# Products of a constant matrix in TensorE's pauses, in a two-layer pair-mixing network with a recurrence and a choice of experts

## The reference, cut to what matters

```python
x = x + _L0_conv_ref(_ln_c(x), ...)   # layernorm, gated projection to 4 x 8 channels, two batched
                                       # 128x128 products per channel, layernorm over 16, gated projection
t = t + _L0_ffn_ref(_ln_t(t), ...)     # Wx, batch statistics, then y = sigmoid(Wx_t + y @ V.T) along the sequence
x = x + _L1_conv_ref(_ln_c(x), ...)   # layernorm, a and b of 32 channels each, 128x128 product per channel,
                                       # layernorm, projection, output gate
t = t + _L1_ffn_ref(_ln_t(t), ...)     # router over 8 experts, softmax, two best, their weighted projections
```

## Time and profile before

| | |
|---|---|
| median of 3 runs | 358.93 us (357.75 to 360.17) |
| the profiled execution | 357.57 us |
| its span, first to last instruction | 355.8 us |
| TensorE busy, of the span | 244.0 us |
| VectorE busy | 248.4 us |
| ScalarE busy | 121.9 us |
| GpSimd busy | 97.5 us |
| mean granted TensorE clock | 0.820 |

### The profile page before, as it was taken

How to read it: one execution, slowest core, us unless ns; L and a number is a source line. 1 busy time by engine, 2 the same in 40 slices (tenths; PEclk the granted TensorE clock), 3 DMA queues, 4 the chain that set the end, 5 groups by cost and what they waited for, 6 DMA issues and landing times.

```text
span 355.8 us, 4549 instructions
## 1 busy us (share of the span) xinstructions
PE 244.0 (69%) x1465; PEld 180.0 (51%) x1465; DVE 248.4 (70%) x467; ACT 121.9 (34%) x224; POOL 97.5 (27%) x137
## 2 busy tenths in 40 slices
PE   1283985747068598970966978934566792989994
PEld 1162774424043498960745758934555791333321
DVE  4997456778867300039997963399799599999994
ACT  3061323324324245622542544642142132121210
POOL 4013363247500393000143671003236313020000
PEclk9996988569659679996798998968596555599999
DMA  7100000000000000000000000000001981096811
GB/s 235 26 2 0 0 2 0 1 1 0 1 0 2 0 0 0 2 3 0 2 0 1 0 0 2 0 0 2 0 1 38 206 200 30 5 204 177 207 59 61
DMA packets 6633, 13.05 MB, mean 37 GB/s; under 512 B 2774, under 2 KB 3030, under 8 KB 6614
## 3 DMA queue, kind: packets, MB, share of 16 engines
q1 hardware_dynamic: 6470, 12.81, 14.2%
q10 hardware_dynamic: 144, 0.01, 0.0%
HBM read 2.32 MB, written 2.10 MB: 12 GB/s over the span
## 4 chain that ended last, share of the span: by engine, by line
PE 44%; DVE 42%; issue 5%; POOL 3%; ACT 3%; DMA 1%; SPq 0%; DVEq 0%; POOLq 0%; ACTq 0%
DVE var L321 6%; DVE sums L313 6%; PE ps L1140 4%; PE ps L798 4%; PE ps L505 4%; PE ps L1120 4%; PE ps L794 4%; DVE xn L494 3%; PE ps L971 2%; PE ps L1050 2%; PE ps L898 2%; PE ps L1036 2%; DVE xn L1586 2%; PE ps L1132 2%; DVE newton L328 1%
## 5 line engine op out<-in xcount | busy, mean ns | idle before, releaser
L505 PE MATMUL ps<-ident,xn 128*128 128x128 f32 x176 | 38.5, 360 | 75.5 <-DVE xn L494 42.4
L505 PEld LDWEIGHTS ps<-ident,xn 128*128 128x128 f32 x176 | 26.9, 186 | 90.0 <-issue 69.9
L679 POOL TENSOR_TENSOR gated<-gated,mask_c x16 | 20.8, 1325 | 57.1 <-DVE gated L1574 57.1
L696 POOL TENSOR_TENSOR x<-x,sg 128x512 f32 x16 | 20.8, 1303 | 45.0 <-DVE sg L1604 43.6
L514 ACT ACTIVATE xt<-ps 128x512 f32<-128x512 f32 (+1 forms) x24 | 12.6, 524 | 49.5 <-PE ps L505 49.4
L321 DVE TENSOR_REDUCE var<-squares 128x32 f32<-128x1024 f32 (+1 forms) x24 | 26.9, 1120 | 0.0
L1120 PE MATMUL ps<-gated,pick 96*128 96x512 bf16 x64 | 21.5, 425 | 2.6 <-ACT gated L1346 1.2
L831 ACT ACTIVATE gated_t<-ps,bn 128x128 f32<-128x128 f32 x56 | 18.1, 366 | 13.4 <-PE ps L798 11.7
L679 POOL TENSOR_TENSOR gated<-gated,mask_a x8 | 10.9, 1357 | 35.2 <-DVE gated L1433 35.2
L317 ACT ACTIVATE squares<-x 128x1024 f32<-128x1024 f32 x16 | 16.7, 1051 | 11.0 <-DVE x L1559 5.9
L313 DVE TENSOR_REDUCE sums<-x 128x32 f32<-128x1024 f32 x16 | 19.3, 1208 | 1.3 <-POOL x L696 1.3
(11 more groups left out here) (254 smaller groups left out, 558.3 us busy)
## 6 DMA issues: line engine op xcount, KB each, us to landing
out_gate<-gated SPq DMA_DIRECT2D x32, 128.0 KB, 2.3
x_copies<-gated SPq DMA_DIRECT2D x32, 128.0 KB, 2.3
x<-in_x_dram SPq DMA_DIRECT2D x4, 512.0 KB, 5.6
out_dram<-x SPq DMA_DIRECT2D x8, 256.0 KB, 2.0
e_full<-in_L_ffn_expert_b_dram SPq DMA_DIRECT2D x12, 1.0 KB
mask_a<-in_L_conv_mask_dram SPq DMA_DIRECT2D x1, 64.0 KB, 6.8
mask_c<-in_L_conv_mask_dram SPq DMA_DIRECT2D x1, 64.0 KB, 1.9
w_x<-in_L_ffn_expert_w_dram SPq DMA_DIRECT2D x1, 32.0 KB
```

Source lines behind the costliest of these rows:

```text
L505: ins = pe.transpose(bank(s)[:, t * P:(t + 1) * P], xn[:, s, t, :], ident[:, :])
L679: pool.tensor_tensor(v, v, m.to_broadcast([P, chans, n]), ALU.mult).then_inc(pj.masked, 1)
L696: pool.tensor_tensor(v, v, sg[:, s, :], ALU.add).then_inc(pj.added, 1)
```

## The change

A function `idle_products(b, n)` is added: n products of `ones_h` (constant, 128 x 128, bf16) with `rows_a` (constant, 256 columns, read twice, so 512 columns), each into the whole of PSUM bank b, which nobody reads before it is written again. It has the form of the bias product in L865. It is called before o and after o's first tail, before b, before c, before and after z and after z's first tail, between the groups of the router, and around the first transposition of the chosen weights. Before o two waits (`pair_a`, `pair_v`) stand ahead of the products, and before c one (`y_added`); before b they stand behind the existing wait for `wv_kept`.

```diff
--- before.py
+++ after.py
@@ -440,12 +440,14 @@
 
         p_a, p_o, p_b, p_c, p_z, p_d = (Proj(n) for n in ("pa", "po", "pb", "pc", "pz", "pd"))
 
-        def groups(eng, head, tail, last=True):
+        def groups(eng, head, tail, pause=None):
 
 
             head(0, 0, True)
             head(1, 1, True)
             tail(0, 0, True)
+            if pause:
+                pause()
             with eng.Fori(1, GROUPS // 2) as it:
                 head(2 * it, 0, False)
                 tail(2 * it - 1, 1, False)
@@ -853,6 +855,13 @@
 
             repeat(bank(7)[:, 0:P], rep32[:, :], rep32[:, :], a_repeated)
             pe.wait_ge(a_built, 1)
+
+            def idle_products(b, n):
+
+                v = rows_a[:, :, :, :].rearrange("p h s o -> p (h s o)").unsqueeze(1)
+                for _ in range(n):
+                    pe.matmul(bank(b).rearrange("p (t n) -> p t n", t=2), ones_h[:, :],
+                              v.to_broadcast([P, 2, 2 * S * C]), start=True, stop=True, skip_group_check=True)
 
             def bias_into(b, key, start=True):
 
@@ -954,7 +963,10 @@
                                         start=False, stop=(t == 1), skip_group_check=True)
                 ins.then_inc(p_o.projected, 1)
 
-            groups(pe, turn_group(pe, p_o, 2), project_o)
+            pe.wait_ge(pair_a, 2)
+            pe.wait_ge(pair_v, 2)
+            idle_products(6, 16)
+            groups(pe, turn_group(pe, p_o, 2), project_o, lambda: idle_products(6, 12))
 
 
             pe.wait_ge(wv_built, 1)
@@ -971,6 +983,7 @@
                 pe.matmul(bank(2 + s), w_bt[:, :], v.rearrange("p a n -> p (a n)"), start=True,
                           stop=True).then_inc(p_b.projected, 1)
 
+            idle_products(7, 20)
             groups(pe, turn_group(pe, p_b), wx)
             pe.wait_ge(bn_dve, 1)
             pe.matmul(bank(4)[:, 0:1], avg4[:, :], mv[:, 0:1], start=True, stop=True).then_inc(bn_pe, 1)
@@ -1038,6 +1051,8 @@
                                             start=False, stop=(t == 1), skip_group_check=True)
                     ins.then_inc(halves, 1)
 
+            pe.wait_ge(y_added, QUARTERS)
+            idle_products(7, 20)
             groups(pe, turn_group(pe, p_c), project_c)
             pe.wait_ge(p_c.masked, 2 * GROUPS)
             def c_products(q):
@@ -1076,7 +1091,9 @@
                                     stop=(t == 3), skip_group_check=True)
                 ins.then_inc(p_z.projected, 1)
 
-            groups(pe, turn_group(pe, p_z), project_z)
+            idle_products(6, 20)
+            groups(pe, turn_group(pe, p_z), project_z, lambda: idle_products(6, 20))
+            idle_products(6, 8)
 
 
 
@@ -1159,9 +1176,12 @@
                 turn(g, g % 2, g < 2)
                 if g:
                     router(g - 1)
+                    idle_products(5, 8 if g == 4 else 2)
             router(GROUPS - 1)
+            idle_products(5, 16)
             turn_weights(0)
             pe.wait_ge(x_mid_kept, 1)
+            idle_products(5, 4)
             for G in range(GROUPS):
                 spread_w(G, 0)
                 bias_e(G)
```

## The result

The changed kernel takes 361.34 us (359.39 to 362.61, 13 runs) beside 358.93 us of the kernel before (357.12 to 360.25, 13 runs): a ratio of 1.0073, with an interval from 1.0053 to 1.0093. It is 2.4 to 2.6 us slower. The profiled execution took 362.61 us, its span is 360.9 us. The clock did come up: the mean granted clock is 0.871, against 0.820, and within the span the low stretches add up to 93.1 us instead of 127.8. Twelve of the changed kernel's thirteen executions have a mean clock of 0.870 or 0.871, so the profiled one is no exception in that; the one with 0.889 is the fastest, 359.39 us. The time went the other way.

The account below looks back on a forecast made before the run. No engine is full; the kernel is a relay, where a faster TensorE counts only where VectorE waits. 357.57 - 1.3 (o) + 0.9 (d) = 357.2, other terms 0; 358.5 against the median 358.93. Own range 356.5 to 360.

Parts of the forecast that it names:

- o: Products ahead of o and behind its first tail: group 1's gate comes earlier, 1.3 us gained (bounds 0 and 1.69).
- b: 20 products ahead of b: 0.8 to 2.1 us late, work then faster by 1.5; net taken as 0.
- c and z: Products before c and around z: VectorE gains and loses nothing; 0 each, up to 0.5 or 2 us lost.
- d: Products in the choice of experts: 1.5 us lost at the exponential, 0.6 won at the weights' spreading; 0.9 lost.
- The exponential: In d, products between the routers delay group 7's transposes and so `exp_d(0)`: 1.5 us lost on VectorE's path.
- The first rival: In d, the clock stays low through the 8 products and groups 5 to 7: 362.3 us; chance 0.2.
- The second: Rival: the clock stays up from z through the whole choice of experts: 355.1 us; chance 0.2.
- 0.6 won back: In d, VectorE's wait for the spread weights (0.8 us at `prod`) shrinks: 0.6 us gained.

Follow-up runs that it names:

- e1: The kernel before with only o's 28 products (16 ahead of o, 12 behind its first tail): 357.58 us, ratio 0.9961.
- e2: The kernel before with only the 20 products ahead of b, behind the wait for `wv_kept`: 360.97 us, ratio 1.0058.
- e10: The kernel before with no products, one more unused VectorE reduction in b's statistics, a delay of 1.27 us: 361.97 us, ratio 1.0081.
- e14: The kernel before with o's 28 products and e12's in d, nothing in b, c, z or between the routers: 357.68 us, ratio 0.9946.
- e8: The kernel before with only the products of c and z (20, and 20 + 20 + 8) and the wait on `y_added`: 359.56 us, ratio 1.0021.
- e6: The kernel before with 10 products instead of 20 ahead of b, nothing else added: 359.10 us, ratio 1.0017.
- e4: The changed kernel without the products of the choice of experts (d), so o, b, c and z only: 357.70 us, ratio 0.9971 against the kernel before.
- e15: The kernel before with all products of d (2 or 8 behind each router, 16 and 4) and 8 more among the first spreadings: 359.90 us, ratio 1.0024.
- e3: The kernel before with only d's products (2 or 8 behind each router, 16 behind the last, 4 at the weight transposes): 361.11 us, ratio 1.0050.
- e12: e7 plus 4 + 4 products in two TensorE pauses among group 0's weight spreadings: 357.38 us, ratio 0.9979 against the kernel before.
- e7: The kernel before with only d's last two calls: 16 products behind the last router, 4 behind the first weight transposes: 363.00 us, ratio 1.0126.
- e13: The changed kernel without the products between the routers and with e12's eight among the spreadings: 357.75 us, ratio 0.9974 against the kernel before.
- e16: The kernel before with no products, two more unused VectorE reductions in b, twice the delay of e10: 362.45 us, ratio 1.0108.
- e11: The kernel before with 46 products ahead of b, placed before the wait for `wv_kept`: 359.04 us, ratio 1.0013.
- e5: The kernel before with 50 products ahead of b, placed before the wait for `wv_kept`: 360.61 us, ratio 1.0082.

## Why the prediction was wrong

**o was right.** 1.3 us forecast, 1.4 measured alone (e1), and the gate's stage is 1.2 shorter.

**b was right in mechanism and its 0 was the wrong size when b stands alone.** The products start 7 us into the pause at 1.2 GHz and take 6.2 to 7.3 us, beside 5.8 to 7.1 forecast. Locally the balance is -0.1 (the change) to +0.8 (e2), inside the forecast's bounds or just over. What the sum left out is what a shift does further on: 2.1 us at the end for 0.8 at the place, and for e10 2.9 for 1.3. The step behind every term, that a local balance reaches the end unchanged, doesn't hold, and the parts that don't add up say the same. The profiles show such changes where nothing is edited: in e14 nothing is added in b, the recurrence or c, yet they changed by +0.47, -0.83 and +1.32. But e8, with no edit ahead of c, has +0.44 and -0.87 there, so a profile alone can't tell the work of a shift from the chance of one execution; the medians carry the argument. It cuts both ways: 1.49 us won in b (e6) came to nothing.

**c and z**: 0 forecast. Alone 1.0021 (0.9997 to 1.0045), so 0.8 us with zero just inside. Within o, b, c and z together (e4) the sum was -1.0 against -1.3 forecast.

**d is the step that failed: +0.9 forecast, 3.7 measured** (the change against e4). In the profiles the change and e4 differ by 0.8 + 1.0 + 1.5 = 3.3 us there, in "router", "spread" and "last". Its terms:
- The exponential. 1.5 us late forecast; 0.80 in the change, 1.98 and 1.99 in e15 and e3. Mechanism and size were about right, and e15 against e12 confirms it over all executions with 1.6 us. The forecast had the clock back 2.5 to 5.2 us after the products' start, where b takes 2.9 to 5.6 from the rows; no row gives the other pair. It was 2.9 us in the change and 5.3 in e3 and e15. The first rival, that the clock doesn't come back in the 8 products and groups 5 to 7 all run low, fell: it was back at 288.3, as they ended, and in e3 and e15 at 290.9 and 289.9, in the router of group 4, right behind group 5's transposes. The second fell too: the clock was low from 271.2, before the choice. The first rival's time, 362.3, lies nearer to the measured 361.34 than the forecast's 358.5, but by another way.
- "0.6 won back" at the weights' spreading, with nothing behind it. What was forecast came: VectorE's first multiplications win 0.51 us in the change and 0.53 in e3, e7, e12, e13 and e15. Then VectorE waits 2.35 us for the spreading that stands behind the 16 fp32 projections, and the stretch as a whole is 1.41 us longer. I followed the clock up to the spreadings, took it as won and put the projections at nothing. In e7 the way is plain: a faster TensorE has longer pauses behind VectorE's multiplications, the clock fell in them and stayed low over the work that does set the pace. e7 has this term and the next one without the exponential, 4.5 us at the end; e12 fills two of the pauses and has both gone. In the change itself the clock fell earlier, at 301.9, behind the wait of 2.71 us for the weights; e3 and e15 have the same wait and kept the clock, so why it fell there is not settled. A row to see e7's way by was at hand: four spreadings take 1.91 us at 1.2 GHz and three biases 0.81 instead of 1.49 at 2.4, while VectorE goes on at its own pace, so TensorE's pauses had to grow there.
- The last projections, 1.53 us more in the change (3.46 us instead of 1.92), 1.56 in e7 and 1.70 in e13. No product was added near them. The clock fell at 353.1 in the change, just as they began, and at 352.7 in e7 and 348.6 in e13; in the kernel before it stayed up until 354.3, after them, and in the profiles of all other kernels they took 1.92 us. That the executions of the change have this more often than those of the kernel before is likely, since nearly all have the mean clock of the profiled one, but it is only argued.

Sum: forecast -1.3 + 0.9 = -0.4; measured -1.0 + 3.7 = +2.7, which is the ratio's 2.6 again but for rounding, since d was taken as the difference; the two medians give 2.4.

**Two rules on the clock.** The rule of the Trainium skill, TensorE: Matmul & The Clock Gate, Part 4 (PE-mode transpose), that transposes don't engage the full clock, would have favoured the first rival, which fell; what failed lies behind that place, so the rule would not have mended the prediction. Over the profiles with the first block unchanged the clock first came up at 18.8 to 22.0 us, and that block took 57.6 to 59.8 us. In the kernel before, the first four products with `w_a` take 1.80 us and the next four 1.03; in the change it is 1.91 and 1.83. The Trainium skill, TensorE: Matmul & The Clock Gate, Part 1 (The HAM clock gate), also says that the number of slow products at the start of one and the same kernel varies from run to run: the trace agrees, and it is a reason why one profile can't be the base of a sum of tenths.

**Open.** Why a delay in b costs about 1.5 us more than itself over all executions is not settled. The mean clocks say that the profiles of e2 and e10 are the usual case of these kernels, with a longer low stretch on the channel products, but not why that is so for them and not for e4. e16's profile doesn't have it (low from 218.4 to 221.8, no longer than before); what it has is +0.36, -0.93 and +1.33 in b, the recurrence and c. Open too are how often the last projections run low in each kernel, and why the clock fell at 301.9 in the change.

## What to carry to other kernels

Filling TensorE's pauses paid in these runs where the fill ended before the real work was ready (o in e1, the tail of d in e12), and cost where it ended late (e2, and the products between the routers) or where it left new pauses behind (e7). Ending in time was not enough: e6 and e11 did, and won nothing at the end. Whether it started at the high clock mattered less: the 16 products of e12 start at 1.2 GHz and end in time. The pauses that the faster TensorE then leaves behind have to be filled too, up to the work that sets the pace (e7 against e12: 5.3 us for eight products, 2.4 of them at the place). Read the clock at the work that someone waits for, not its mean: the mean rose from 0.820 to 0.871 and the kernel got slower. And in a relay kernel with many low stretches, test each part alone and together, over many executions: stages that no edit touches differ by up to 1.5 us from profile to profile.

## What the runs showed of the hardware that was not expected

- A stop of TensorE for its own code. With 50 added products (e5) it stood 2.72 us in the middle of the transposes of y, behind a sweep of the recurrence that is a loop; a queue of instructions moved one block of 16 KB in that stretch. The kernel before and e11 have such a block in the same stretch and no stop, so the block alone doesn't tell. With 46 (e11) there was no stop: four products fewer, some 55 us earlier, decide over 2.7 us. That it is the place of the code in its blocks is inferred; no run moved the code and left the products alone. The waits of TensorE in e5:

```profile
PE ps L1002 <- issue: 3.0, 2, 2.7
```

- The same pause lets the clock fall in one kernel's profile and not in another's: the last projections follow a wait of 1.32 us everywhere, and ran low in three profiles of eighteen. The return varies too: it took 2.9 us of work in one profile and 6.0 in another for the same channel products (e10), and in the change 9.39 us of work within 9.90, from 301.9 on, did not bring it.
